# Two of a turn's 36 gathers replaced by columns copied on VectorE and ScalarE

## The chip, the cores and the metric

One core of a Trainium2 chip runs the whole program in one launch. The metric is the device time of one execution in microseconds. The kernel before takes 4103.11 us, the median of three runs (4102.42 to 4103.65).

## The reference

Two layers of a graph network over 6,250 nodes with 128 features and 206,250 directed edges, which are sorted by destination. The second layer, the convolution, is the one that the change is about. `src` and `dst` come from the inputs, so which rows are read is known only at run time.

```
h = max(layernorm(x), 0)
x = x + attention_layer(h, edge_index, edge_type, node_type, ...)     # layer 0: softmax over edges, 3 edge types
h = max(layernorm(x), 0)
filters    = silu(edge_attr @ fW1 + fb1) @ fW2 + fb2                  # per edge, 50 -> 128 -> 128
messages   = (h[src] @ dW + db) * filters                             # per edge
aggregated = segment_sum(messages, dst)                               # per node
x = x + (h + silu(aggregated @ uW1 + ub1) @ uW2 + ub2)
```

## The kernel before, in words

Edges are cut into chunks of 128 (one edge per partition), six chunks make a unit of 768 edges, six units make a turn. There are 269 units in 45 turns, the last of five units. Both layers run over the same turns, the attention layer first (`attention_edges`, line 721), then the convolution (`convolution_edges`, line 1300).

In the convolution the product `h @ dW + db` is not computed per edge. The attention layer's last steps write it, a row of 128 floats per node, to a table in HBM (`messages`, later `table`, line 799). It goes there 128 nodes at a time: once a turn from the third on, TensorE turns the tile of h (its features onto the partitions, `p.turned`, line 1079) and multiplies it by `dW`, VectorE adds `db` (line 1082, into the same buffer). The last seven tiles follow at the stage's end (line 814).

GpSimd then gathers, chunk by chunk, the rows of the 128 sources of a chunk into `xg` with one indirect DMA (`gather`, line 62, from `gather_units`, line 688): `xg` has a place for each of the six units of a turn, and a place is filled again as soon as VectorE has used it (`xg_free`, which is `s_msg`). Only one chunk in two turns (20 in all) doesn't come so: SyncE fetches its 128 rows by 128 single DMAs into a staging buffer (`Carry.collect`, lines 609 to 617) and moves them into the sixth chunk of unit 4. SyncE also loads the source indices, three units at a time (`load_indices`, line 620), after the units that used the old ones have landed.

The other engines in the convolution, per unit: TensorE makes the hidden layer (line 1441, two matmuls into `ps_h`), ScalarE applies silu (line 1387), TensorE makes the filters (line 1417, six matmuls into one of two PSUM banks), VectorE adds the bias `fb2` (line 1490) and multiplies by the gathered rows (line 1496), TensorE sums by destination (line 1426, with a one-hot that VectorE makes at line 1484), and VectorE adds the sums to the accumulator (line 1504). TensorE issues the hidden layer of unit n, then the filters of n-1, then the sums of n-3. Once a turn a finished tile of 128 nodes goes through the update layer (lines 1386, 1415, 1524, 1527) and out to HBM. ScalarE also issues the loads of the edge attributes, two a turn (line 1370). Each engine's order is written out by hand; nothing is planned at run time.

VectorE reads the window bases of a turn into registers by one load of ten values (line 500). The six loads of the residual `y` (448 KB each) are issued by SyncE in turn 0 (line 1354), three behind each index load.

Of the kernel before, what the change touches and what calls it, by code (L numbers as in the profile page):

```python
# [496 lines left out]

def bases(nc, engine, h, first, count):
# [40 lines left out]

LOAD = 3  # L540
# [15 lines left out]
def landed_by(pace, r, i, s, carried=0, j=0):  # L556
# [63 lines left out]
def load_indices(nc, sp, a, h, idx, idx_in, gathered, landed, carry, xg, xg_free, ahead=lambda r, i, v: None, beside=lambda r, i: None,  # L620
                 behind=lambda r, i: None, listed=lambda: None):
# [22 lines left out]
    def span(r, t, b, first=False):  # L644

        for q in range(span_turns * LOADS):
            j, v = divmod(q, LOADS)
            following(r, span_turns * t + j, v)
            if q == 0 and not first:
                deliver(r, t, b)  # L650
            if q == 0 and first:
                listed()
# [35 lines left out]
def gather_units(pool, passes, table, xg, width, idx, idx_in, gathered, xg_free, pool_turn, carry):  # L688
# [32 lines left out]
def attention_edges(nc, h, a, acc, state, typ, table, messages, sent, y, project, sources, following):  # L721

    with ExitStack() as ctx:
# [23 lines left out]
        landed, pool_turn, steps, key_ready, begun, rise_zero = (  # L747
            sem(k) for k in "landed pool_turn steps key_ready begun rise_zero".split())
# [32 lines left out]
        def _(sp):  # L781
# [21 lines left out]
            sp.sem_inc(stored, 32)  # L803
            load_indices(nc, sp, a, h, idx, idx_in, gathered, landed, carry, xg, s_sum, beside=beside, behind=behind)
# [4 lines left out]
            sp.wait_ge(stored, 32 * (passes * DONE + 1))  # L809
            first_indices(sp, a, following.idx, following.idx_in)  # L810
            for n, k in enumerate((1, 0)):
                a0, a1 = HALVES[k]
                sp.wait_ge(t_hdc, n + 1)
                sp.dma_start(messages[(LAST + a0) * P:(LAST + a1) * P, :].rearrange("(t p) r -> p t r", p=P), l_hd[:, a0:a1, :]).then_inc(last_stored, 16)
            sp.wait_ge(last_stored, 32)

        @block.gpsimd
        def _(pool):
            gather_units(pool, project.pool_passes, table, xg, ROW, idx, idx_in, gathered, s_sum, pool_turn, carry)
# [18 lines left out]
        def _(act):  # L838
            nc.scalar.copy(acc[:, 1:NT, 0:NP], acc[:, 0, 0:NP].unsqueeze(1).to_broadcast([P, NT - 1, NP]))
            with act.Fori(0, pass_count(act, h)) as r:  # L840
# [55 lines left out]
                def relus(k):  # L896

                    act.wait_ge(stored, 32 * k)
# [162 lines left out]
        def _(dve):  # L1061
# [9 lines left out]
            with dve.Fori(0, pass_count(dve, h)) as r:  # L1071
                def tile(i, s):
# [4 lines left out]
                    if closes(i) and s == 1:  # L1077
                        dve.wait_ge(stored, 32 * (r * DONE + i - OPEN))
                        nc.vector.tensor_copy(p.turned, ps_c[:, P:2 * P])
                        nc.vector.tensor_tensor(p.relu, p.rows, p.relu, ALU.add)  # L1080
                    if closes(i) and s == 2:
                        nc.vector.tensor_tensor(p.turned, ps_c[:, 2 * P:3 * P], p.db, ALU.add)
# [180 lines left out]
class Project:  # L1263


    def __init__(self, nc, ctx):
        sb = lambda name, shape: ctx.enter_context(nc.sbuf_tensor("pj_" + name, shape, fp32))
        self.w, self.dw, self.bias = sb("w", [P, NT, D]), sb("dw", [P, D]), sb("bias", [P, NT, D])
        parts = sb("parts", [P, 3, D])
        self.relu, self.turned, self.db = (parts[:, k, :] for k in range(3))  # L1270
# [4 lines left out]
        self.carry_turn = ctx.enter_context(nc.semaphore("pj_carry_turn"))  # L1275
        self.raise_from = self.tile[:, :, 0:TILES]
# [23 lines left out]
def convolution_edges(nc, h, a, acc, update, table, sent, sources, project, y, out):  # L1300

    with ExitStack() as ctx:  # L1302
# [17 lines left out]
        sem_landed = sem("landed")  # L1320
# [4 lines left out]
        (w_in, pool_turn, steps, key_ready, begun, cleared, s_hid, s_act, s_flt, s_bias, s_msg, s_sum, s_acc) = (  # L1325
            sem("c_" + k) for k in "w_in pool_turn steps key_ready begun cleared hid act flt bias msg sum acc".split())
# [6 lines left out]
        def _(sp):  # L1333
# [5 lines left out]
            update.load(sp, a)  # L1339

# [14 lines left out]
            load_indices(nc, sp, a, h, sources.idx, sources.idx_in, gathered, sem_landed, carry, xg, s_msg, attributes, beside=beside, listed=lambda: sp.wait_ge(scaled, 1))  # L1355
# [8 lines left out]
        def _(act):  # L1364
            act.wait_ge(w_in, 64)
            act.wait_ge(update.loaded, 64)
            with act.Fori(0, pass_count(act, h)) as r:
# [5 lines left out]
                def turn(i, first, count):  # L1373
                    for s in range(count):
# [6 lines left out]
                        if opens(i) and s == 1:  # L1381
                            k = r * DONE + i - OPEN
                            act.wait_ge(t_u, k + 1)
                            if not (isinstance(i, int) and i == OPEN):
# [3 lines left out]
                                             ACT.Silu, bias=fb1[:, :]).then_inc(s_act, 1)  # L1388
                finishing_turns(act, turn)
# [5 lines left out]
        @block.gpsimd  # L1395
        def _(pool):
            gather_units(pool, project.pool_passes, table, xg, D, sources.idx, sources.idx_in, gathered, s_msg, pool_turn, carry)

        @block.tensor
        def _(pe):  # L1400
            pe.sem_inc(s_hid, XS)
            pe.wait_ge(w_in, 64)
            pe.wait_ge(update.loaded, 64)
            with pe.Fori(0, pass_count(pe, h)) as r:
                def filters(n, s, fresh, i=None):
# [7 lines left out]
                    if i is not None and opens(i) and s == UPDATE_SLOT:  # L1413
                        pe.wait_ge(t_hid, r * DONE + i - OPEN + 1)
                        nc.tensor.matmul(tile_y, one_hid[:, :], update.w2[:, :], start=True, stop=True).then_inc(t_v, 1)
                    for c in range(CH):
# [3 lines left out]
                def sums(n, s, fresh, count=CH):  # L1420
# [6 lines left out]
                    last.then_inc(s_sum, 1)  # L1427

                def turn(i, first, count):
                    for s in range(count):  # L1430
# [12 lines left out]
                        if not (first and s < 1):  # L1443
                            filters(n - 1, (s - 1) % SL, first and s < 3, i if s else None)
# [27 lines left out]
        def _(dve):  # L1472
            dve.sem_inc(s_msg, XS)
            nc.vector.memset(h.sweep[:, :], 0.0).then_inc(cleared, 1)
# [6 lines left out]
            with dve.Fori(0, pass_count(dve, h)) as r:  # L1481
# [5 lines left out]
                def messages(n, s, i, carried, j=0):  # L1487
# [3 lines left out]
                    if s == UPDATE_SLOT and opens(i):  # L1491
                        update_tile(i)
                    dve.wait_ge(s_bias, n)
                    carry.landed(dve, r, s, carried)
                    dve.wait_ge(gathered[s], landed_by(carry.pace, r, i, s, carried, j))
# [10 lines left out]
                def turn(i, first, count, carried, j=0):  # L1506
                    back = 0 if first else 4
                    base = bases(nc, mybir.EngineType.DVE, h, i * SL - back, count - 4 + back)
                    for s in range(count):
# [3 lines left out]
                        if not (first and s < 1):  # L1513
                            one_hot(i * SL + s - 1, v)
                            messages(n - 1, v, i if s else i - 1, carried, j)
# [49 lines left out]
def program(nc, a, out):  # L1565
    table0 = nc.dram_tensor("table0", (NP, ROW), fp32).ap()
    sent = nc.dram_tensor("sent", (DONE * P, D), fp32).ap()
    table1 = nc.dram_tensor("table1", (NP, D), fp32).ap()
    with ExitStack() as ctx:
# [4 lines left out]
        with ExitStack() as banks:  # L1574
            with nc.sbuf_tensor("state", [P, NT, NW], fp32) as state, nc.sbuf_tensor("typ", [P, NU, CH], bf16) as typ:
                prepare(nc, h, a, sums, state, typ, table0, project, attention_sources)
                project.ring = banks.enter_context(nc.psum_tensor("ring", [P, 2048], fp32))
                attention_edges(nc, h, a, sums, state, typ, table0, table1, sent, y, project, attention_sources, sources)
        update = Update(nc, ctx)
        messages = sums[:, 0, :]  # L1580
        convolution_edges(nc, h, a, messages, update, table1, sent, sources, project, y, out)
# [43 lines left out]
```

## Time and profile before

| | us |
|---|---|
| median of three runs | 4103.11 |
| the profiled execution: its span, first to last instruction | 4098.5 |
| what lies around the span (4103.11 less 4098.5) | 4.6 |
| attention gathers, GpSimd | from 61.7 |
| convolution, first gather to the last sum | 2091.9 to 4090.9 |
| GpSimd busy, whole span | 3050.9 (74%) |
| TensorE busy | 3358.1 (82%) |
| VectorE busy | 2405.1 (59%) |
| ScalarE busy | 1368.9 (33%) |

Busy counts the instructions of the engines themselves; register loads and arithmetic, waits and the issue of DMAs are not in it. The profile has no time of its own for the execution beside its span, so 4.6 us is taken as what lies around it.

### The profile page before, as it was taken

Reading aid. Unit: us, or ns where it says so; the run is one execution under the profiler, and the core shown is the slowest. Engines: PE = TensorE matmul, PEld = TensorE weight load, DVE = VectorE, ACT = ScalarE, POOL = GpSimd, SP = SyncE. Lnnn points to the kernel's source line nnn. Section 1 sums busy time; section 2 is a strip of 40 time slices with the busy share of each in tenths; the row PEclk is TensorE's granted clock in tenths of the full one; section 3 lists DMA queues with packets and bytes.
Section 4 is the critical chain, followed back from the end, with each engine's and each line's share of the span. In section 5 each row is a group of like instructions: output and inputs, shape, how many; then the busy total and the mean of one; then the engine's idle time right before and its main releaser. Section 6 shows DMA issues by size and latency. Waiting matters only on the chain. (4 is left out here: it accounts for less than half of the span.)

```text
span 4098.5 us, 63699 instructions
## 1 busy us (share of the span) xinstructions
PE 3358.1 (82%) x14005; PEld 2625.3 (64%) x14006; DVE 2405.1 (59%) x5327; ACT 1368.9 (33%) x3398; POOL 3050.9 (74%) x3216
## 2 busy tenths in 40 slices
PE   5788888888888888888768898888888888888798
PEld 3566666666666666666656676766766666666676
DVE  7888888888888888888853333333333332333333
ACT  5455555555555555555421111111111111111111
POOL 6777777777777777777757777777777777777776
PEclk7555555555555555555567666667666677667767
DMA  4222222222222222222232222222222222222222
GB/s 125 58 60 61 61 60 61 62 60 61 61 60 61 61 61 60 61 61 59 59 88 78 79 74 78 79 74 78 75 77 78 75 78 78 74 79 74 78 78 62
DMA packets 190049, 288.10 MB, mean 70 GB/s; under 512 B 85904, under 2 KB 132811, under 8 KB 185384
## 3 DMA queue, kind: packets, MB, share of 16 engines
q0 software_dynamic: 101888, 212.13, 20.6%
q1 hardware_dynamic: 83160, 33.99, 3.5%
q10 hardware_dynamic: 4840, 40.55, 3.2%
q14 instruction: 147, 1.20, 0.1%
q8 instruction: 14, 0.23, 0.0%
HBM read 271.07 MB, written 12.49 MB: 69 GB/s over the span
## 5 line engine op out<-in xcount | busy, mean ns | idle before, releaser
L63 POOL DMA_INDIRECT ce_xg<-table,ce_idx x1592 | 1509.2, 948 | 491.6 <-issue 481.5
L63 POOL DMA_INDIRECT ae_xg<-table,ae_idx x1592 | 1502.5, 944 | 491.2 <-issue 489.6
L1496 DVE TENSOR_TENSOR ce_msg<-ce_ring,ce_xg 128x768 f32<-128x768 f32 x269 | 257.6, 958 | 1151.0 <-DMA ce_xg<-table,ce_idx 1150.6
L948 PE MATMUL ae_ps_k<-ae_xg,ae_e 128*96 128x129 f32 x3224 | 882.7, 432 | 0.0
L1417 PEld LDWEIGHTS ce_ring<-ce_fw,ce_hid 128*128 128x128 f32 x3228 | 586.6, 278 | 435.6 <-DVE ce_msg L1496 314.6
L1417 PE MATMUL ce_ring<-ce_fw,ce_hid 128*128 128x128 f32 x3228 | 649.6, 377 | 262.1 <-DVE ce_msg L1496 261.8
L948 PEld LDWEIGHTS ae_ps_k<-ae_xg,ae_e 128*96 128x96 f32 x3224 | 689.6, 277 | 126.7 <-issue 117.2
L1387 ACT ACTIVATE ce_hid<-ce_ps_h,ce_fb 128x768 f32<-128x768 f32 x269 | 241.8, 899 | 1235.4 <-PE ce_ps_h L1441 692.2
L1441 PE MATMUL ce_ps_h<-ce_ea,ce_fw 50*128 50x384 f32 x1076 | 548.3, 641 | 19.0 <-DMA ce_ea<-in_edge_attr 17.1
L1426 PEld LDWEIGHTS ce_ring<-ce_hot,ce_msg 128*128 128x128 f32 x3224 | 528.4, 253 | 3.0 <-DVE ce_msg L1496 2.9
L1426 PE MATMUL ce_ring<-ce_hot,ce_msg 128*128 128x32 f32 x3224 | 514.3, 319 | 1.0 <-DVE sums L1504 1.0
L868 ACT ACTIVATE ae_off<-cst,plan 128x96 bf16<-128x96 f32 x1614 | 454.1, 363 | 5.0 <-DVE plan L491 5.0
L860 ACT ACTIVATE ae_upper<-ring 128x576 f32<-128x576 f32 x269 | 174.9, 650 | 668.3 <-DVE ring L1125 668.3
L996 PE MATMUL ring<-ae_rise,cst 64*128 64x192 f32 x538 | 270.4, 605 | 84.2 <-DVE ae_rise L1148 81.2
L963 PE MATMUL ae_ps_tz<-cst,ae_high 128*96 128x128 f32 x269 | 120.7, 449 | 251.8 <-DVE ae_high L1135 251.8
L1441 PEld LDWEIGHTS ce_ps_h<-ce_ea,ce_fw 50*128 50x128 f32 x1076 | 227.2, 234 | 145.1 <-issue 65.8
L1135 DVE TENSOR_REDUCE ae_high<-ae_e 128x96 f32<-128x576 f32 x269 | 304.8, 1133 | 0.0
L1490 DVE TENSOR_TENSOR ce_ring<-ce_ring,ce_fb 128x768 f32<-128x768 f32 x269 | 258.3, 960 | 71.5 <-PE ce_ring L1417 71.2
L1125 DVE TENSOR_TENSOR ring<-ring,ae_xg 128x576 f32<-128x576 f32 x269 | 206.1, 766 | 126.0 <-DMA ae_xg<-table,ae_idx 122.3
L963 PEld LDWEIGHTS ae_ps_tz<-cst,ae_high 128*96 128x96 f32 x269 | 41.9, 156 | 316.6 <-DVE ae_high L1135 316.6
L996 PEld LDWEIGHTS ring<-ae_rise,cst 64*128 64x128 f32 x538 | 134.0, 308 | 171.4 <-DVE ae_rise L1148 158.2
L844 ACT ACTIVATE ae_e<-ae_e 128x576 f32<-128x576 f32 x269 | 183.7, 683 | 105.6 <-DVE ae_e L1157 105.5
(186 smaller groups left out, 3336.2 us busy)
## 6 DMA issues: line engine op xcount, KB each, us to landing
ae_stage<-table SPq DMA_DIRECT2D x2560, 0.5 KB
ce_stage<-table SPq DMA_DIRECT2D x2560, 0.5 KB
ce_ea<-in_edge_attr ACTq DMA_DIRECT2D x88, 450.0 KB
ae_xg<-table,ae_idx POOLq DMA_INDIRECT x1592, 2.5
ce_xg<-table,ce_idx POOLq DMA_INDIRECT x1592
sums<-in_x SPq DMA_DIRECT2D x7, 448.0 KB, 4.6
table<-sums SPq DMA_DIRECT2D x6, 462.0 KB, 3.5
pj_bias<-in_x_rows SPq DMA_DIRECT2D x42, 64.0 KB
```

The source lines that it names most:

```text
L63: eng.indirect_dma_start(out=out, out_offset=None, in_=table[:, :], in_offset=bass.IndirectOffsetOnAxis(ap=idx, axis=0)).then_inc(done, 16)
L868: last = nc.scalar.activation(off[:, s % 2, c, :], h.iota, ACT.Square, bias=keys[:, c:c + 1], scale=STEP)
L948: last = nc.tensor.matmul(ps_k[0:KEYS, 0:D + 1], by_chunk[s % 3][:, c, :], xg[:, s % XS, c, 0:D + 1], start=(c == 0), stop=(c == count - 1))
L996: nc.tensor.matmul(ps_m[s % 2][:, 0:2 * KEYS], h.raised_by[0:64, :], rise[:, :, :].rearrange("p a k -> p (a k)"), start=True, stop=True).t ...
L1125: nc.vector.tensor_tensor(by_kind, by_kind, xg[:, s % XS, :, D + 1:ROW].unsqueeze(3).to_broadcast([P, CH, NT, W]), ALU.add).then_inc(s_ful ...
L1135: nc.vector.tensor_reduce(out=high[:, :], in_=by_chunk[s % 3].rearrange("p c k -> p k c"), op=ALU.max, axis=AX.X).then_inc(s_high, 1)
L1387: nc.scalar.activation(hid[:, b, :].rearrange("p (k e) -> p k e", k=2), ps_h[:, :].rearrange("p (k e) -> p k e", k=2)[:, :, 0:H], ACT.Silu ...
L1417: last = nc.tensor.matmul(ps_f[b][:, c * D:(c + 1) * D], hid[:, b, c * P:(c + 1) * P], fw2[:, :], start=True, stop=True)
L1426: last = nc.tensor.matmul(ps_a[s % 2][:, 0:W], msg[:, s % 3, c, :], hot[:, s % 3, c, :], start=(c == 0), stop=(c == count - 1))
L1441: last = nc.tensor.matmul(ps_h[:, k * 512:k * 512 + H], fw1[:, :], ea[:, s // LOAD, q:q + H], start=True, stop=True)
L1490: nc.vector.tensor_tensor(filt, filt, fb2[:, :].unsqueeze(1).to_broadcast([P, CH, D]), ALU.add).then_inc(s_bias, 1)
L1496: nc.vector.tensor_tensor(msg[:, s % 3, :, :], filt, xg[:, s % XS, :, :], ALU.mult).then_inc(s_msg, 1)
```

## The change

In the convolution the sixth chunk of units 1 and 3 is no longer gathered in turns 2 to 44. Its h @ dW + db is computed afresh on the chip. For it h itself, turned, is written to HBM in the attention layer (`features`, [128, 6272] floats, one more DMA a turn and one at the end) and loaded whole into SBUF as `by_node` (3.2 MB, 25,088 bytes a partition) in turn 0 of the convolution. A source's h is then one column of `by_node`.

In each of turns 1 to 43, two blocks `held[:, m, :]` of 128 columns are filled: m = 0 in units 0 to 2 for unit 1 of the next turn, m = 1 in units 3 to 5 for unit 3. VectorE copies columns 0 to 47 (16 in each of three units), ScalarE columns 48 to 127 (28, 28 and 24). Each copy is an instruction of one element a partition, whose source address comes from a register; the registers are loaded from a list in SBUF (`columns`), up to 16 values by one load. TensorE multiplies the block by `dW` (one matmul of 128 columns), and VectorE adds `db` and writes the sum into `xg`.

```
+def sources_at(nc, engine, columns, i, m, first, end):
+    for e in range(first, end, PIECE):                      # PIECE = 16
+        yield from nc.values_load_multi_w_load_instructions(columns[32 * m:32 * m + 1, bass.ds((i - 1) * P + e, min(PIECE, end - e))], engines=[engine], ...)[1]

+COLUMNS = (Column((0, 1, 2), 5, 1), Column((3, 4, 5), 2, 3))    # collected in units, multiplied at, goes to unit
+COLUMN_TURNS = TURNS - 2
+HALF = 48

 gather_units:
-                taken = carried is not None and s == CARRY_SLOT
+                taken = carried is not None and s == CARRY_SLOT or s in to and not (isinstance(i, int) and i < 2)

 attention, SyncE:
-                    sp.dma_start(messages[bass.ds((i - OPEN - 1) * P, P), :], p.turned).then_inc(stored, 16)
+                    sp.dma_start(messages[bass.ds((i - OPEN - 1) * P, P), :], p.message).then_inc(stored, 16)
+                    sp.dma_start(features[:, bass.ds((i - OPEN - 1) * P, P)], p.turned).then_inc(stored, 16)
 ...
+            for ready in (t_ht, t_first_ht):
+                sp.wait_ge(ready, 1)
+            sp.dma_start(features[:, LAST * P:NP].rearrange("f (t p) -> f t p", p=P), l_ht).then_inc(project.last_turned, 16)

 convolution, SyncE, in turn 0 behind the first index load:
+            def tables(r):
+                sp.wait_ge(scaled, 1)
+                sp.wait_ge(project.last_turned, 16)
+                sp.wait_ge(s_column, r * COLUMN_TURNS * len(COLUMNS) + len(COLUMNS))
+                sp.dma_start(by_node, features[:, :]).then_inc(table_in, 16)

 convolution, ScalarE, behind the silu of each unit of turns 1 to 43:
+                def collect(i, s):
+                    e0, e1 = column.batch(s, HALF, P)
+                    if s == column.collected[0]:
+                        act.wait_ge(s_column, column_at(r, i, m) + 1)
+                    if s == 0:
+                        act.wait_ge(table_in, 16 * (r + 1 + len(COLUMNS)))
+                    for k, node in enumerate(sources_at(nc, mybir.EngineType.Activation, columns, i, m, e0, e1), e0):
+                        last = nc.scalar.copy(held[:, m, k:k + 1], by_node[:, bass.ds(node, 1)])
+                    if s == column.collected[-1]:
+                        last.then_inc(s_other, 1)

 convolution, TensorE, ahead of a unit's filters:
+                def products(i, m, b):
+                    pe.wait_ge(s_half, k + 1)
+                    pe.wait_ge(s_other, k + 1)
+                    nc.tensor.matmul(ps_x[b], held[:, m, :], project.dw[:, :], start=True, stop=True).then_inc(s_column, 1)

 convolution, VectorE, in messages(), between the bias and the multiplication by xg:
+                def collect(i, s):          # as ScalarE's, columns 0 to HALF, nc.vector.tensor_copy, s_half
+                def place(i, m, b):
+                    dve.wait_ge(s_column, column_at(r, i, m) + 1 + len(COLUMNS))
+                    dve.wait_ge(s_msg, r * UNITS + i * SL + column.to + 1 + XS)
+                    nc.vector.tensor_tensor(xg[:, column.to, CH - 1, :], ps_x[b], project.db, ALU.add).then_inc(s_placed, 1)
 ...
+                    for m, to in enumerate(TO):
+                        if s == to and not (isinstance(i, int) and i < 2):
+                            dve.wait_ge(s_placed, column_at(r, i - 1, m) + 2)
```

## Rows read from the trace of the kernel before

**Rows 1.** The page: busy time by engine, and the chain that ended last.
```profile
PE 3358.1 (82%) x14005; PEld 2625.3 (64%) x14006; DVE 2405.1 (59%) x5327; ACT 1368.9 (33%) x3398; POOL 3050.9 (74%) x3216
...
POOL 35%; issue 12%; DMA 1%; POOLq 1%; DVE 0%; PE 0%; ACT 0%; DVEq 0%
```

**Rows 2.** Timeline of POOL, 40 gathers apart: start us, duration us, instruction [idle before].
```profile
2999.86 0.94 POOL L63 DMA_INDIRECT ce_xg<-table,ce_idx  x1 [0.30 <-issue]
...
3049.83 0.95 POOL L63 DMA_INDIRECT ce_xg<-table,ce_idx  x1 [0.30 <-issue]
```

**Rows 3.** Groups of instructions on POOL, whole span.
```profile
L63 POOL DMA_INDIRECT ce_xg<-table,ce_idx x1592 | 1509.2, 948 | 491.6 <-issue 481.5 <-DVEq L1473 6.5 <-DVE ce_msg L1496 3.3
```

**Rows 4.** Who waited for whom, 2100 to the end: us, times, longest.
```profile
DVE ce_msg L1496 <- DMA ce_xg<-table,ce_idx: 1150.6, 264, 10.3
ACT ce_hid L1387 <- PE ce_ps_h L1441: 692.2, 144, 13.5
```

**Rows 5.** Busy time by engine in one turn: PE, PEld, DVE, ACT, POOL, clock, DMA.
```profile
3000.00:3044.30 44.30, 39.78 (x181) 31.15 (x180) 14.00 (x26) 6.56 (x8) 33.61 (x36) 0.69 0.30 82
```

**Rows 6.** Groups on DVE and ACT, 2200 to 4050 us.
```profile
L1524 DVE TENSOR_TENSOR ce_done<-sums,up_b 128x128 f32<-128x128 f32 x42 | 12.3, 293 | 77.8 <-DMA out_x<-ce_done 77.8
...
L1387 ACT ACTIVATE ce_hid<-ce_ps_h,ce_fb 128x768 f32<-128x768 f32 x250 | 224.7, 899 | 1145.2 <-PE ce_ps_h L1441 607.1 <-issue 538.1
```

**Rows 7.** Timeline of DVE: one unit, then a turn's start.
```profile
3020.20 0.96 DVE L1496 TENSOR_TENSOR ce_msg<-ce_ring,ce_xg 128x768 f32<-128x768 f32 x1 [7.78 <-DMA ce_xg<-table,ce_idx]
3021.07 0.18 DVE L1504 TENSOR_TENSOR sums<-sums,ce_ring 128x32 f32 x1
3021.17 0.35 DVE L1484 TENSOR_TENSOR ce_hot<-cst,key 128x192 f32<-128x192 f32 x1
3021.44 0.96 DVE L1490 TENSOR_TENSOR ce_ring<-ce_ring,ce_fb 128x768 f32<-128x768 f32 x1
3023.20 0.96 DVE L1496 TENSOR_TENSOR ce_msg<-ce_ring,ce_xg 128x768 f32<-128x768 f32 x1 [0.80 <-DMA ce_xg<-table,ce_idx]
3025.46 0.19 DVE L1504 TENSOR_TENSOR sums<-sums,ce_ring 128x32 f32 x1 [1.30 <-issue]
```

**Rows 8.** Register loads, by line: ns min/median/max, first and last start.
```profile
L500 DVEq TENSOR_LOAD <-base_i x1: 1412/1412/1412, 3023.7 to 3023.7; - x1
...
L500 DVEq TENSOR_LOAD <-base_i x46: 556/901/1429, 2109.7 to 4083.0; - x46
...
L613 SPq TENSOR_LOAD <-ce_lists x160: 1132/1208/1696, 2126.1 to 3881.8; - x160
```

**Rows 9.** Line 868 for one unit: sequencer's register work, and its instructions.
```profile
L868 ACTq FUSED_REGOPS  x6: 46/46/60, 1003.0 to 1003.6; - x6
```

**Rows 10.** Timeline of ACT: an activation of one column, and the next.
```profile
1000.56 0.20 ACT L894 ACTIVATE pj_few<-pj_few 128x1 f32<-128x1 f32 x1
1000.67 0.24 ACT L855 COPY ae_by_key<-ae_ps_k 96x129 f32<-96x129 f32 x1
```

**Rows 11.** Line 1146, a copy on DVE with a source address from a register.
```profile
L1146 DVE COPY ae_rise<-state x269: 240/241/243, 85.2 to 2058.5; 1x96 f32 x135
```

**Rows 12.** Groups on DVE: the shortest instruction.
```profile
L442 DVE MEMSET pr_eps<- 128x1 f32 x1 | 0.1, 59 | 0.0
```

**Rows 13.** Line 1370, the issue of ScalarE's attribute loads.
```profile
L1370 ACTq DMA_DIRECT2D ce_ea<-in_edge_attr x83: 731/738/763, 2208.9 to 4029.3; - x83
```

**Rows 14.** Timeline of SP in the convolution's first turns.
```profile
2124.39 1.68 SPq L1354 DMA_DIRECT2D sums<-sent  x3
2127.41 13.09 SPq L617 DMA_DIRECT2D ce_stage<-table  x32
2143.55 0.61 SPq L631 DMA_DIRECT2D ce_idx<-in_src  x1
```

**Rows 15.** Timeline of POOL: unit 3 of turn 1.
```profile
2147.78 0.94 POOL L63 DMA_INDIRECT ce_xg<-table,ce_idx  x1 [0.30 <-DMA ce_idx<-in_src]
```

**Rows 16.** Window behind the first loads of y, columns as in Rows 5, then GB/s.
```profile
2125.00:2130.00 5.00, 5.00 (x22) 4.63 (x22) 2.53 (x5) 0.14 (x1) 3.77 (x4) 0.50 0.89 237
```

More of the change, by code:

```diff
@@ L537, in __init__, with batch, collects, places @@
         self.chunks = (span * SL * np.arange(1, carried + 1) + CARRY_SLOT) * CH + CH - 1
+class Column:
+    def __init__(self, collected, placed, to):
+        self.collected, self.placed, self.to = collected, placed, to
+        self.late = placed < collected[-1]
+    def batch(self, s, e0, e1):
+        q, parts, fours = self.collected.index(s), len(self.collected), (e1 - e0) // 4
+        return e0 + 4 * -(-fours * q // parts), e0 + 4 * -(-fours * (q + 1) // parts)
+COLUMNS = (Column((0, 1, 2), 5, 1), Column((3, 4, 5), 2, 3))
+COLUMN_TURNS = TURNS - 2
+TO = [column.to for column in COLUMNS]
+HALF = 48
+PIECE = 16
+STORES = 48
+def collects(i):
+    return not (isinstance(i, int) and not 1 <= i <= COLUMN_TURNS)
+def places(i, column):
+    first = 2 if column.late else 1
+    return not (isinstance(i, int) and not first <= i < first + COLUMN_TURNS)
+def column_chunks():
+    turn = np.arange(2, TURNS)
+    return np.concatenate([(turn * SL + to) * CH + CH - 1 for to in TO])
+def column_at(r, i, m):
+    return r * COLUMN_TURNS * len(COLUMNS) + (i - 1) * len(COLUMNS) + m
 LOAD = 3
@@ L818, in _ @@
         def _(pool):
-            gather_units(pool, project.pool_passes, table, xg, ROW, idx, idx_in, gathered, s_sum, pool_turn, carry)
+            gather_units(pool, project.pool_passes, table, xg, ROW, idx, idx_in, gathered, s_sum, project.pool_turn, carry)
             pool.wait_ge(last_in, 16)
@@ L1297, with convolution_edges @@
 UPDATE_SLOT = 3
-def convolution_edges(nc, h, a, acc, update, table, sent, sources, project, y, out):
+def convolution_edges(nc, h, a, acc, update, table, features, by_node, sent, sources, project, y, out):
     with ExitStack() as ctx:
@@ L1324, in convolution_edges @@
         carry = Carry(sb, lambda name: sem("c_" + name), CONVOLUTION, D, project, lists, table)
-        (w_in, pool_turn, steps, key_ready, begun, cleared, s_hid, s_act, s_flt, s_bias, s_msg, s_sum, s_acc) = (
-            sem("c_" + k) for k in "w_in pool_turn steps key_ready begun cleared hid act flt bias msg sum acc".split())
+        (w_in, steps, key_ready, begun, cleared, s_hid, s_act, s_flt, s_bias, s_msg, s_sum, s_acc) = (
+            sem("c_" + k) for k in "w_in steps key_ready begun cleared hid act flt bias msg sum acc".split())
+        columns = sb("columns", [P, COLUMN_TURNS * P], i32)
+        held = sb("held", [P, len(COLUMNS), P])
+        ps_x = [ps_f[b][:, 1024 - P:1024] for b in range(2)]
+        table_in, s_half, s_other, s_column, s_placed = (sem("x_" + k) for k in "table_in half other column placed".split())
         merged, out_done, y_in, s_u, s_up_hid, s_v, s_up_bias, s_y = (sem("f_" + k) for k in "merged out_done y_in u hid v bias y".split())
@@ L1415, in filters @@
                         nc.tensor.matmul(tile_y, one_hid[:, :], update.w2[:, :], start=True, stop=True).then_inc(t_v, 1)
+                    for m, column in enumerate(COLUMNS):
+                        if at is not None and at[1] == column.placed and places(at[0], column):
+                            products(at[0] - 1 if column.late else at[0], m, b)
                     for c in range(CH):
@@ L1443, in turn @@
                         if not (first and s < 1):
-                            filters(n - 1, (s - 1) % SL, first and s < 3, i if s else None)
+                            filters(n - 1, (s - 1) % SL, first and s < 3, i if s else None, (i, s))
                         if not (first and s < 3):
@@ L1485, in one_hot, with aside, messages @@
                                             keys.unsqueeze(2).to_broadcast([P, CH, W]), ALU.is_equal)
-                def messages(n, s, i, carried, j=0):
+                def collect(i, s):
+                    m = next(m for m, column in enumerate(COLUMNS) if s in column.collected)
+                    column = COLUMNS[m]
+                    e0, e1 = column.batch(s, 0, HALF)
+                    if s == column.collected[0]:
+                        dve.wait_ge(s_column, column_at(r, i, m) + 1)
+                        dve.sem_inc(begun, 1)
+                    if s == 0:
+                        dve.wait_ge(table_in, 16 * (r + 1 + len(COLUMNS)))
+                        dve.sem_inc(begun, 1)
+                    for k, node in enumerate(sources_at(nc, mybir.EngineType.DVE, columns, i, m, e0, e1), e0):
+                        last = nc.vector.tensor_copy(held[:, m, k:k + 1], by_node[:, bass.ds(node, 1)])
+                    if s == column.collected[-1]:
+                        last.then_inc(s_half, 1)
+                def place(i, m, b):
+                    column = COLUMNS[m]
+                    dve.wait_ge(s_column, column_at(r, i, m) + 1 + len(COLUMNS))
+                    dve.wait_ge(s_msg, r * UNITS + i * SL + column.to + 1 + XS)
+                    nc.vector.tensor_tensor(xg[:, column.to, CH - 1, :], ps_x[b], project.db, ALU.add).then_inc(s_placed, 1)
+                def aside(r, at):
+                    if at is None:
+                        return
+                    i, s = at
+                    for m, column in enumerate(COLUMNS):
+                        if s == column.placed and places(i, column):
+                            place(i - 1 if column.late else i, m, (s - 1) % SL % 2)
+                    if collects(i):
+                        collect(i, s)
+                def messages(n, s, i, carried, j=0, at=None):
                     filt = ps_f[s % 2][:, 0:CH * D].rearrange("p (c f) -> p c f", c=CH)
```

66 lines of the change are left out of this document (43 added, 23 removed).

## The prediction

> **What bounds the kernel now.** I read the page first. TensorE is busiest by share, but the chain that ended last is 35% GpSimd and 12% "issue", and nothing else has over 1% [rows 1]. The reader should see that busy shares mislead here: the chain lies on GpSimd's indirect DMAs. The timeline of GpSimd says why: gathers follow each other with 0.94 us busy and 0.30 us "issue" between, and 40 of them take 49.97 us, so 1.249 us each [rows 2]. Over the whole convolution this hardly breaks: of 491.6 us of idle time before 1592 gathers, 481.5 are that issue time and 3.3 are waits for VectorE to free a place [rows 3]. The waits say the same from the other side: VectorE waits 1150.6 us for gathered rows, ScalarE 692.2 us for TensorE, which itself is held up by VectorE [rows 4]. So a turn costs 35.5 gathers (36, less one every second turn) x 1.249 = 44.3 us, and every other engine follows.
>
> **What is removed.** Units 1 and 3 lose one gather each in turns 2 to 44: 86 gathers x 1.249 = 107.4 us. A turn becomes 33.5 x 1.249 = 41.8 us. All of it is on the path, as long as no other engine needs over 41.8 us a turn. That is the whole question, and I work out each engine's turn.
>
> **ScalarE, 80 x 2 = 160 copies a turn.** No such copy is in the trace. An instruction whose address comes from a register first takes register work of the sequencer: six at line 868 start within 0.6 us though each takes 0.046, so one every 0.12 to 0.13 us, the dispatch included [rows 9]. On the engine itself an activation of one column lasts 0.20 us and the next starts 0.11 us after it [rows 10]. Low end 0.11, high end 0.20 (no overlap). I take 0.13, since the sequencer feeds no faster: 160 x 0.13 = 20.8. Register loads: two per unit, 16 values and 12 (8 in every third). SyncE's loads of 16 have a median of 1.21, VectorE's of ten 0.90 [rows 8]; so 1.21 + 0.90 = 2.1 a unit, 12.7 a turn. Two attribute loads are issued at 0.74 [rows 13], with their registers 1.7. The update tile, loop and semaphore waits: I allow 1.6. Sum 36.8 us. The six silus of 0.90 [rows 6], 5.4 us, run on the engine while the sequencer loads the next registers: on VectorE a load started at 3023.7 [rows 8] while the multiplication of 3023.20 to 3024.16 still ran [rows 7]. Without that cover it is 42.2, just over GpSimd's turn. With 0.20 a copy, its loads and silus not hidden: 32 + 12.7 + 5.4 + 3.3 = 53.4.
>
> **VectorE, 48 x 2 = 96 copies.** Its bounds lie further apart: 0.06 (the one-column memset) [rows 12] and 0.24 (a copy with a register address, 96 elements on one partition) [rows 11]. I take 0.13 as on ScalarE: 12.5 us. Six loads of 16 at 1.21: 7.3. Today's work by start spacing: 0.87 + 0.10 + 0.27 + 0.96 = 2.2 a unit, 13.2 a turn [rows 7]. Base load 1.4, update tile 0.6 plus its wait for the store before, 77.8 / 42 = 1.9 [rows 6], two `place` additions 0.6. Sum 37.5 us with nothing overlapped, against 41.8. At 0.24 a copy it would be 48.1, which is over.
>
> The copies stand ahead of the multiplication by `xg`. What is queued behind them is that multiplication; for it wait TensorE's sums and GpSimd's next gather into the place, six units on. A unit's 3.3 us come while rows are still landing, where VectorE idles 7.8 us in one unit and 0.8 in the next [rows 7]. GpSimd's lead of several units takes up the uneven landing.
>
> **TensorE.** Two more matmuls of 128 columns a turn. It is busy 39.8 of 44.3 us at a granted clock of 0.69, between its two levels of 1.2 and 2.4 GHz [rows 5]. The same work must now fit into 41.8; at 0.69 it does, with about 0.8 us for the two: 40.6. The new waits there (`s_half`, `s_other`) are for units collected two to three units earlier, and cost nothing. Cover is thin: at a mean clock of 0.60 it would need about 47.
>
> **SyncE and the beginning.** In turn 0 the 3.2 MB of `by_node` go behind the first three loads of `y` and ahead of the staging rows. Those 1.34 MB are mostly in a window of 5 us at 237 GB/s, the gathers' bytes included [rows 16]. At 240 to 350 GB/s the table takes 9 to 13 us more, in which gathers hardly land. The index load for unit 3 of turn 1 waits for unit 5 of turn 0 to land; it was issued at 2143.55 and GpSimd needed it just as it came, at 2147.78, with no more than the usual 0.30 between gathers [rows 14, 15]. Any delay there goes straight to the path. I estimate 3.5 us: gathers held until about 2142, then a backlog of some 5 us. VectorE's and ScalarE's wait for the table at turn 1 is behind that and within GpSimd's lead. Low end 0, high end 13.
>
> In the attention layer SyncE gets one more DMA a turn (about 0.4 us) while GpSimd sets the pace, so nothing; at its end two waits and one more DMA stand ahead of the last wait for the stores: 1 us. The renamed and shared semaphores cost nothing.
>
> **The sum.** Span 4098.5 - 107.4 + 3.5 + 1.0 = 3995.6; with 4.6 us around it 4000.2. The profiled execution has no other time of its own, and by this account it equals the median of 4103.11. So **4000 us, 2.5% faster**.
>
> A rule of the Trainium skill weighs against the VectorE part. First the rows: the copy at line 1146, float from SBUF to SBUF, took 240 to 243 ns in all 269 cases [rows 11] beside a GpSimd that was busy three quarters of the time, so none of them waited for a gather's 0.94 us. "SBUF — State Buffer", section "SBUF: two separate sides", says that a VectorE copy in a two-port mode and GpSimd's descriptor writing exclude each other for a whole instruction. By the rule the new copies would queue behind gathers; by the row they don't. Another, "VectorE: DVE Perf Modes", section "The TRN2 errata", gives a ScalarE instruction from SBUF to SBUF 224 cycles at 1.2 GHz; 160 x 0.19 = 30 us a turn would, as an estimate by that page, bring ScalarE to about 46, where the overlap in rows 10 says less.
>
> **Rivals.**
> *(a) Part of the gain is lost (0.13).* ScalarE or VectorE need 42 to 44 us a turn: silus uncovered (42.2), or code for 160 copies fetched anew each turn. Each us over 41.8 costs 43: at 43 us a turn 4000 + 52 = 4052. For it: the thin margins above. Against: 5 us of margin on ScalarE, 4 on VectorE.
>
> *(b) ScalarE becomes the bound (0.09), slower.* A one-column copy takes its full 0.20 us and nothing hides the loads: 53.4 us a turn, (53.4 - 44.3) x 43 = +391, so 4494. With the loads hidden it is about 44 to 46 and the time 4100 to 4180. It decides from (44.3 - 12.7 - 5.4 - 3.3) / 160 = 0.143 us a copy without cover. For it: no row shows one of these copies. Against: rows 9 and 10.
>
> *(c) VectorE's copies and GpSimd's gathers take turns (0.06), slower.* Copies run only in the 0.30 us between gathers [rows 2]. At 0.06 each [rows 12] five fit, so 16 need four gaps, 5.0 us; with 1.2 and 2.2 a unit takes 8.4, a turn 50.4: +262, so 4365. Against: rows 11.
>
> *(d) Nothing changes (0.03)*: one engine happens to need 44 to 44.5 us.
>
> The forecast has 0.69. **Range and chances.** The forecast's own range is 3994 (no delay at the beginning, a little overlap gained) to 4013 (the full 13 us). Reaching into (a) up to 4085 holds about eight in ten: 3993 to 4085. About 0.2% (8 us) is what a measurement of this kernel tells from no change. Faster: the forecast and nearly all of (a), 0.81; same 0.04; slower, (b) and (c), 0.15.
>
> **What would show it.** Line 63 in the convolution has 1506 gathers and still 1.249 us between them, with no new releaser. ScalarE's and VectorE's copies start 0.11 to 0.14 us apart within a batch. VectorE's wait for gathered rows falls from 1150 us to 200 to 500 but doesn't vanish; if it is near zero and GpSimd waits for line 1496's successor, (a), (b) or (c) holds, and the copies' spacing tells which: over 0.14 on ScalarE is (b), copies on VectorE that start in clusters after gathers end is (c). One idle stretch of GpSimd before unit 3 of turn 1 is the table's price. The prediction is wrong if a turn of GpSimd takes over 42.5 us.

## The result, and the profile after

The changed kernel takes 3995.99 us (median of four runs, 3994.69 to 3998.18) against 4103.38 us of the kernel before beside it: a ratio of 0.9736, with a 95% interval of 0.9723 to 0.975. Its profiled execution spans 3994.3 us, 104.2 less than the 4098.5 before.

The page after, busy times and the chain of waits, which answer to [rows 1]:
```profile
PE 3385.6 (85%) x14177; PEld 2645.2 (66%) x14178; DVE 2914.9 (73%) x9541; ACT 2120.9 (53%) x10279; POOL 2970.5 (74%) x3130
...
POOL 32%; issue 11%; DMA 2%; DVE 1%; POOLq 1%; DVEq 1%; PE 0%; SPq 0%
```
VectorE and ScalarE are busy for 1262 us more in sum (509.8 and 752.0), and the chain is still GpSimd's (in c0_after's profile, further down, 23% GpSimd and 11% TensorE). The costliest groups that answer to [rows 3, 6, 7], from the page:
```profile
L63 POOL DMA_INDIRECT ce_xg<-table,ce_idx x1506 | 1429.0, 949 | 465.6 <-issue 454.0
L1473 ACT COPY ce_held<-sums 128x1 f32 x6880 | 751.9, 191 | 329.3 <-issue 325.2
...
L1598 DVE COPY ce_held<-sums 128x1 f32 x4128 | 507.5, 153 | 118.7 <-issue 117.8
```
1592 gathers have become 1506, of unchanged length. Their timeline, 40 gathers apart, answers to [rows 2] (start, duration, instruction, idle before):
```profile
2998.64 0.94 POOL L63 DMA_INDIRECT ce_xg<-table,ce_idx  x1 [0.30 <-issue]
...
3048.74 1.09 POOL L63 DMA_INDIRECT ce_xg<-table,ce_idx  x1 [0.30 <-issue]
```
50.10 us for 40, against 49.97 before; one gather of 1.09 us at 3006.13 in place of 0.94 makes up all of the difference. One turn answers to [rows 5]; the columns are the same:
```profile
3000.00:3041.80 41.80, 36.09 (x172) 28.78 (x172) 24.75 (x118) 23.50 (x173) 31.73 (x34) 0.74 0.31 80
```
Who waited for whom, 2095 us to the end, answers to [rows 4]:
```profile
ACT ce_hid L1456 <- issue: 381.6, 120, 6.3
...
DVE ce_msg L1633 <- DMA ce_xg<-table,ce_idx: 298.2, 109, 7.5
DVE sums L1641 <- issue: 170.1, 41, 6.0
ACT ce_hid L1456 <- PE ce_ps_h L1539: 118.0, 54, 10.1
```
VectorE's wait for gathered rows fell from 1150.6 us to 298.2. It is the room that the new copies use: it shrank and did not vanish. GpSimd's waits for VectorE to free a place stay at 4.0 us from 2200 to 3800 us, 3.3 before. ScalarE's timeline over most of a turn shows how the copies come:
```profile
3003.80 0.90 ACT L1456 ACTIVATE ce_hid<-ce_ps_h,ce_fb 128x768 f32<-128x768 f32 x1
3005.03 1.71 ACT L1473 COPY ce_held<-sums 128x1 f32 x16 [0.32 <-issue]
3007.54 1.30 ACT L1473 COPY ce_held<-sums 128x1 f32 x12 [0.81 <-issue]
3008.90 1.27 ACTq L1439 DMA_DIRECT2D ce_ea<-in_edge_attr  x1
...
3014.26 0.90 ACT L1473 COPY ce_held<-sums 128x1 f32 x8 [0.56 <-issue]
3018.96 0.90 ACT L1456 ACTIVATE ce_hid<-ce_ps_h,ce_fb 128x768 f32<-128x768 f32 x1 [3.81 <-issue]
```
Sixteen copies of 0.19 us take 1.71 us together: each starts (1.71 - 0.19) / 15 = 0.101 us after the one before. Between batches stands what is left of a register load, 0.81 us. At the turn's end ScalarE stands still for 3.81 us with nothing but "issue" as the reason. VectorE's timeline of one unit:
```profile
3001.82 0.96 DVE L1623 TENSOR_TENSOR ce_ring<-ce_ring,ce_fb 128x768 f32<-128x768 f32 x1
3002.69 1.92 DVE L1598 COPY ce_held<-sums 128x1 f32 x16
3005.08 0.96 DVE L1633 TENSOR_TENSOR ce_msg<-ce_ring,ce_xg 128x768 f32<-128x768 f32 x1 [0.47 <-DMA ce_xg<-table,ce_idx]
```
Here the spacing is (1.92 - 0.15) / 15 = 0.118 us, right through two of GpSimd's gathers:
```profile
3002.39 0.94 POOL L63 DMA_INDIRECT ce_xg<-table,ce_idx  x1 [0.30 <-issue]
3003.64 0.94 POOL L63 DMA_INDIRECT ce_xg<-table,ce_idx  x1 [0.30 <-issue]
```

**Where the 104.2 us come from.** 86 gathers give 107.4. Against it stand the first gather, 0.74 us later than before (2092.68 for 2091.94), 1.6 us more between the last gather's start and the end (14.7 us, from 3979.58, for 13.1 from 4085.35), and 0.9 us of small irregularities between gathers. In a second profiled execution of the same kernel (c0_after below) the last gather starts at 3977.77 of a span of 3990.9, so 13.1 us again. In e1, e2, e3, e5 and e9 it is 13.5 to 14.8, with 14.8 in e1, which has none of the one-column copies: it varies from one execution to the next, and the 1.6 can't be put down to the change.

### The profile page after: what moved, and what is told of

It reads as the page before. It is cut to its first block and busy times, and to the rows that moved or that the text cites. A ratio compares the mean times of both kernels' runs of the same rounds, so it can differ in the third digit from the quotient of the medians.

```text
span 3994.3 us, 88540 instructions
## 1 busy us (share of the span) xinstructions
PE 3385.6 (85%) x14177; PEld 2645.2 (66%) x14178; DVE 2914.9 (73%) x9541; ACT 2120.9 (53%) x10279; POOL 2970.5 (74%) x3130
## 5 line engine op out<-in xcount | busy, mean ns | idle before, releaser
L63 POOL DMA_INDIRECT ce_xg<-table,ce_idx x1506 | 1429.0, 949 | 465.6 <-issue 454.0
L1473 ACT COPY ce_held<-sums 128x1 f32 x6880 | 751.9, 191 | 329.3 <-issue 325.2
L1508 PEld LDWEIGHTS ce_ring<-ce_fw,ce_hid 128*128 128x128 f32 x3228 | 594.9, 281 | 156.3 <-issue 90.8
L1598 DVE COPY ce_held<-sums 128x1 f32 x4128 | 507.5, 153 | 118.7 <-issue 117.8
L1539 PE MATMUL ce_ps_h<-ce_ea,ce_fw 50*128 50x384 f32 x1076 | 561.5, 655 | 34.0 <-DMA ce_ea<-in_edge_attr 19.1
L1517 PEld LDWEIGHTS ce_ring<-ce_hot,ce_msg 128*128 128x128 f32 x3224 | 509.7, 245 | 6.2 <-DVE ce_msg L1633 2.9
L1517 PE MATMUL ce_ring<-ce_hot,ce_msg 128*128 128x32 f32 x3224 | 496.7, 312 | 4.1 <-DVE sums L1641 2.5
L1633 DVE TENSOR_TENSOR ce_msg<-ce_ring,ce_xg 128x768 f32<-128x768 f32 x269 | 257.6, 958 | 305.1 <-DMA ce_xg<-table,ce_idx 298.2
L1018 PEld LDWEIGHTS ae_ps_tz<-cst,ae_high 128*96 128x96 f32 x269 | 41.8, 155 | 320.3 <-DVE ae_high L1190 320.3
```

What stands on the lines that cost most here:

```text
L63: eng.indirect_dma_start(out=out, out_offset=None, in_=table[:, :], in_offset=bass.IndirectOffsetOnAxis(ap=idx, axis=0)).then_inc(done, 16)
L1473: last = nc.scalar.copy(held[:, m, k:k + 1], by_node[:, bass.ds(node, 1)])
L1508: last = nc.tensor.matmul(ps_f[b][:, c * D:(c + 1) * D], hid[:, b, c * P:(c + 1) * P], fw2[:, :], start=True, stop=True)
L1517: last = nc.tensor.matmul(ps_a[s % 2][:, 0:W], msg[:, s % 3, c, :], hot[:, s % 3, c, :], start=(c == 0), stop=(c == count - 1))
L1539: last = nc.tensor.matmul(ps_h[:, k * 512:k * 512 + H], fw1[:, :], ea[:, s // LOAD, q:q + H], start=True, stop=True)
L1598: last = nc.vector.tensor_copy(held[:, m, k:k + 1], by_node[:, bass.ds(node, 1)])
```

## The experiments

The kernel before ran beside each: 4102.77 us (13 runs, 4099.38 to 4107.8) beside the first eight, 4102.16 in one run beside the last two. Where no interval is given a kernel ran once.

**c0_after: the changed kernel again.** No edit.

> The changed kernel again, timed on the same chip as the three runs beside it. Theory (GpSimd sets the pace, 86 gathers of 1.249 us are gone, all else is hidden): 3996 us, within 3 us. Rival (part of the 107.4 us is given back by slower turns, which varies from run to run): more than 5 us of scatter.

Measured 3993.74 us (3991.11 to 3995.28), ratio 0.9731 [0.9714, 0.9747].

**e1_block: the copies without their addresses.** Each batch becomes one copy of a fixed block, without register loads. The messages of the two chunks are then not their sources'.
```
-                    for k, node in enumerate(sources_at(nc, ..., columns, i, m, e0, e1), e0):
-                        last = nc.scalar.copy(held[:, m, k:k + 1], by_node[:, bass.ds(node, 1)])
+                    last = nc.scalar.copy(held[:, m, e0:e1], by_node[:, e0:e1])      # and so on VectorE
```


> The register loads and the 256 one-column copies a turn are left out: each engine copies its share of a block in one instruction, columns 0 to 127 of the table in place of the sources' (so the messages of those two chunks are not those of their sources). Waits, matmuls, additions and dropped gathers stay. Theory (the copies and loads are hidden entirely): 3994 to 3997, no faster than with them; the jump back at a turn's end falls from 2.75 us (VectorE) and 3.2 to 4.0 us (ScalarE) to some 0.1 us, since the turn's code is short again; the last gather to the end is back at 13.2 us from 14.8. Rival (they cost part of the gain): 3970 to 3990.

Measured 3996.64 us (3994.89 to 3999.79), ratio 0.974 [0.9724, 0.9757]: the same as with all 256 copies. Everything that they cost lies beside GpSimd's work. The end did not come back to 13.2 us as expected, it is 14.8. Groups of this kernel, then of the changed one, 2200 to 3800 us, show what became of the stall at a turn's end, which falls before VectorE's addition of the sums:
```profile
L1639 DVE TENSOR_TENSOR sums<-sums,ce_ring 128x32 f32 x229 | 41.0, 179 | 47.7 <-issue 36.8 <-PE ce_ring L1516 10.8
```
```profile
L1641 DVE TENSOR_TENSOR sums<-sums,ce_ring 128x32 f32 x229 | 41.1, 180 | 168.4 <-issue 168.4
```
Before the change this "issue" is mostly the base load (1.30 us a turn in [rows 7]), and so it is here: 36.8 us over 38 turns is 1.0 a turn. In the changed kernel it is 168.4 / 38 = 4.4. So 3.4 us a turn on VectorE come with the 96 copies and six loads in the loop's body and go with them. The records of the sequencers where the changed kernel's loop jumps back show where it lies (within 3000 to 3042 us; count, ns, first and last start):
```profile
L526 ACTq COMPARE_BRANCH  x1: 54/54/54, 3015.0 to 3015.0; - x1
L526 ACTq FUSED_REGOPS  x1: 119/119/119, 3018.7 to 3018.7; - x1
...
L627 DVEq COMPARE_BRANCH  x2: 55/59/63, 3020.2 to 3020.3; - x2
L627 DVEq MOVE  x2: 36/40/43, 3023.1 to 3023.2; - x2
```
Behind the jump back ScalarE's sequencer does nothing for 3.6 us and VectorE's for 2.8. In e1 neither of them pauses there for over 0.3 us, from 2200 to 3800. The page lists a DMA queue of the kind "instruction" (packets, MB, share of the engines); the changed kernel, then e1:
```profile
q14 instruction: 547, 4.48, 0.4%
```
```profile
q14 instruction: 156, 1.28, 0.1%
```
The kernel before has 147. So 400 packets of 8 KB come with the copies and go with them. In the changed kernel four packets lie in ScalarE's pause (3015.3 to 3019), two in VectorE's idle stretch (3021 to 3025.8), none from 3003 to 3015. That each pause is a fetch of the loop's code fits count, time and place; the queue's row doesn't say which engine a packet is for, so that last step is argued.

**e2_kept: the new work, and the gathers too.** GpSimd gathers all 36 chunks again, and the sum with `db` goes to a tile that nothing reads.
```
-gather_units(..., project.pool_turn, carry, TO)
+gather_units(..., project.pool_turn, carry)
-nc.vector.tensor_tensor(xg[:, column.to, CH - 1, :], ps_x[b], project.db, ALU.add)
+nc.vector.tensor_tensor(aside_x[:, :], ps_x[b], project.db, ALU.add)
```


> All the new work is done, but GpSimd gathers all 1592 chunks and the computed messages go to a tile that nobody reads. Theory (adds nothing to a turn of 44.3 us): before plus 0.7 us at the convolution's beginning plus up to 1.6 at its end, 4104 to 4106. Rival (the new work slows GpSimd's gathers or starves a unit now and then): 4110 or more.

Measured 4102.09 us (4100.06 to 4106.82, 10 runs), ratio 0.9999 [0.9989, 1.0008]. The table's write and load, 256 copies, two products and two additions a turn cost nothing that can be measured; all the gain is the removed gathers.

**e3_one: one column instead of two.**
```
-COLUMNS = (Column((0, 1, 2), 5, 1), Column((3, 4, 5), 2, 3))
+COLUMNS = (Column((0, 1, 2), 5, 1),)
```


> Only the first of the two chunks is taken from GpSimd (unit 1's; units 3 to 5 copy nothing). Theory: 43 gathers of 1.249 us go, 53.7 us, less 0.8 us at the beginning and up to 1.6 at the end: 4050 to 4052. Rival (a first column is free, a second pays partly): below 4047, since then the first one brings more than half.

Measured 4048.61 us (4046.55 to 4054.66), ratio 0.9863 [0.9846, 0.9879]. The first column gives 54.2 us, the second another 54.9, against 43 gathers of 1.249 = 53.7 each; e3's own runs lie 8 us apart. The gain is linear in gathers up to here.

**e4_act_twice and e5_dve_twice: every copy made twice, on one engine.** In e4 on ScalarE (320 a turn), in e5 on VectorE (192).
```
+for to in (twice, held):
+    last = nc.scalar.copy(to[:, m, k:k + 1], by_node[:, bass.ds(node, 1)])      # e5: nc.vector.tensor_copy
```


> ScalarE copies each of its columns twice (the first time into a tile that nobody reads): 320 copies a turn, the register loads unchanged. The changed kernel's trace has 16 of its copies in 1.71 us, so 0.10 each, and a ScalarE turn of about 36 us with the jump back. Theory (0.10 a copy, sequencer and engine overlapped): 36 + 16 = 52 us a turn, so (52 - 44.3) x 43 above before: about 4440. Rival one (the 0.13 of the prediction): 57.6 us, about 4670. Rival two (a copy's full 0.19 us, if nothing overlapped): 67 us, about 5080.

> VectorE copies each of its columns twice (once into a tile that nobody reads): 192 copies a turn. In the trace 16 take 1.92 us, 0.118 each, and a unit takes 4.0 us of VectorE. Theory: 31 + 11.3 = 42 us a turn, on the edge of GpSimd's 41.8: 3996 to 4020. Rival (VectorE's turn is already nearly full, the 37.5 of the prediction without overlap): 49 us, about 4300.

Measured: e4 4022.83 us, e5 3999.86. e5 is inside what was expected, though not for the reason given; e4 is a plain miss, by some 400 us. Its timeline of ScalarE:
```profile
3002.13 0.19 ACT L1475 COPY ce_twice<-sums 128x1 f32 x1
3002.23 0.19 ACT L1475 COPY ce_held<-sums 128x1 f32 x1
3002.32 0.19 ACT L1475 COPY ce_twice<-sums 128x1 f32 x1
```
and its groups, 2200 to 3800 us:
```profile
L1475 ACT COPY ce_held<-sums 128x1 f32 x5986 | 1110.5, 188 | 0.0
L1475 ACT COPY ce_twice<-sums 128x1 f32 x5986 | 1110.4, 188 | 78.6 <-issue 71.0
```
Copies now start every 0.093 us on average, and the idle time before them is 78.6 us where the changed kernel has 288.8 in the same window. The second copy of a source needs no new address. ScalarE's sequencer gets ahead of its engine, and does the loads and address work of the next copies while the engine still works the old ones off. So the two don't add up, the longer one counts: the expectation had charged a doubled copy like a new one. GpSimd did lose here: the turn went from 41.8 to 41.8 + (4022.8 - 3993.7) / 43 = 42.5 us, with ScalarE waiting almost only for itself (busy 1334.85 of 1600 us, the fourth engine in the row below). By this it is the sequencer that sets ScalarE's turn in the changed kernel, not the copies' execution.
```profile
2200.00:3800.00 1600.00, 1425.46 (x6597) 1127.25 (x6597) 983.76 (x4641) 1334.85 (x12234) 1203.56 (x1274) 0.71 0.31 80
```
e5's timeline of VectorE shows the same there:
```profile
2999.87 0.15 DVE L1600 COPY ce_twice<-sums 128x1 f32 x1
2999.94 0.14 DVE L1600 COPY ce_held<-sums 128x1 f32 x1
3000.02 0.15 DVE L1600 COPY ce_twice<-sums 128x1 f32 x1
```
From 2200 to 3800 its copies start 0.076 us apart on average, the changed kernel's 0.120. 192 x 0.076 is 14.6 us and 96 x 0.120 is 11.5: the doubling cost some 3 us a turn and not the 11.3 of the expectation, so VectorE was never at the edge, and the hit is luck.

**e6_half16 and e7_half96: the split between the engines.** Sources, addresses and loads move with the copies.
```
-HALF = 48
+HALF = 16        # e7: 96
```


> Another split: VectorE copies 16 columns of a block, ScalarE 112. ScalarE's turn gains 64 copies at 0.10 and six more register loads (18 in all; 5.6 us): 36 + 12 = 48 us. Theory: ScalarE becomes the bound, (48 - 44.3) x 43 above before, 4260 within 60. Rival (ScalarE's loads are hidden by its engine's backlog): 43 us a turn, 4050.

> The other way: VectorE copies 96 columns of a block (32 a unit, two loads), ScalarE 32. VectorE's turn gains 96 copies at 0.118 and six loads at 1.1: 31 + 18 = 49 us. Theory: VectorE becomes the bound, 4300 within 60; ScalarE idles. Rival (the loads are hidden under the bias addition): 43 to 45 us a turn, 4050 to 4130.

Measured: e6 4242.57 us, e7 4405.48. e6 hit, e7 came 45 us beyond its upper end. The waits of e6, then of e7, 2200 to 3800 us:
```profile
DVE ce_ring L1623 <- PE ce_ring L1508: 900.7, 198, 9.5
ACT ce_held L1473 <- issue: 401.7, 667, 1.1
...
POOL ce_xg L63 <- DVE ce_msg L1633: 202.0, 123, 3.5
...
PE ce_ps_h L1539 <- ACT ce_hid L1456: 137.0, 81, 3.5
```
```profile
ACT ce_hid L1456 <- PE ce_ps_h L1539: 517.4, 93, 10.9
...
DVE ce_held L1598 <- issue: 309.1, 365, 1.2
...
POOL ce_xg L63 <- DVE ce_msg L1633: 298.9, 104, 6.6
```
In both, GpSimd now waits for VectorE to free a place (202.0 and 298.9 us; [rows 3] had 3.3). In e6 VectorE is not the cause, for it waits 900.7 us for TensorE's filters; TensorE in turn waits for ScalarE's silus, which stand behind 224 copies a turn, and ScalarE's own idle time is nearly all "issue"; in e7 VectorE has 192 copies and waits for next to nothing. A turn is 44.3 + (4242.6 - 4102.8) / 43 = 47.6 us on ScalarE, and 44.3 + (4405.5 - 4102.8) / 43 = 51.3 on VectorE. From the changed kernel's estimated 36 and 31 that is 11.6 us for 64 copies and six loads on ScalarE (18 loads a turn for 12; by 0.101 and 0.81: 11.3), and 20.3 for 96 copies and six loads on VectorE (by 0.118 and 1.1: 17.9). The 36 is borne out, the 31 was too low. From 2200 to 3800 us, 38.3 turns, the changed kernel's VectorE waits for TensorE and DMAs for 324.5 us:
```profile
DVE ce_msg L1633 <- DMA ce_xg<-table,ce_idx: 226.6, 84, 7.5
...
DVE ce_ring L1623 <- PE ce_ring L1508: 81.1, 45, 3.7
DVE ce_done L1661 <- DMA out_x<-ce_done: 16.8, 16, 7.2
```
That is 8.5 us a turn and leaves 33.3 of 41.8; 33.3 + 17.9 = 51.2 is what e7 took. Sixteen copies also often take longer than the 1.92 us above, as in e7:
```profile
3006.77 2.04 DVE L1598 COPY ce_held<-sums 128x1 f32 x16 [1.20 <-issue]
```
This isn't e7's own, the changed kernel has the like:
```profile
3027.76 2.04 DVE L1598 COPY ce_held<-sums 128x1 f32 x16 [0.55 <-issue]
```

**e8_three and e9_half64: is there anything left to win?** e8 takes three columns of two chunks, with 56 copies each on VectorE; e9 keeps two with an even split.
```
-COLUMNS = (Column((0, 1, 2), 5, 1), Column((3, 4, 5), 2, 3))
+COLUMNS = (Column((0, 1), 4, 0), Column((2, 3), 1, 1), Column((4, 5), 2, 3))
-HALF = 48
+HALF = 56        # e9: COLUMNS as it was, HALF = 64
```


> Three columns of two chunks each in place of two of three: 384 copies a turn for 256, and one gather a turn fewer on GpSimd (33.3 for 34.3 with the rest). The first 56 copies of a column are VectorE's, 72 ScalarE's. If GpSimd were still what ends a turn, the turn would be 41.8 - 1.25 = 40.6 us, and the time about 3994 - 43 x 1.25 = 3940. If the turn is what the copying engines can bear, VectorE goes from 31 us by 72 copies of 0.118, six register loads of 1.1 and one more placing of 0.3 to 46.4, and ScalarE from 36 by 56 copies of 0.10 and five loads of 0.8 to 45.6, besides what they wait for each other: a turn of 46 to 49, a time of 4103 + 43 x (47.5 - 44.3) = 4240, between 4170 and 4310.

> The same two columns, with 64 copies of each on VectorE and 64 on ScalarE (48 and 80 in the changed kernel): 32 copies and two register loads a turn more on VectorE, as many fewer on ScalarE. VectorE's turn goes from 31 to 31 + 32 x 0.118 + 2 x 1.1 = 37.0 us, ScalarE's from 36 to 31.2, both below GpSimd's 41.8. If GpSimd sets the time, this is 3994, within 6. If either copying engine set part of it, the time would move by 43 turns times what the split shifts: 43 x 1 us a turn is 43 us, and under 3980 or over 4020 would be read so.

Measured: e8 4277.77 us, a turn of 48.4; e9 3997.99; both are inside what was expected. The split can move by 16 columns to VectorE without effect; a third column costs far more than its gather. e9 did more than its expectation says: VectorE has six register loads a turn more (516 in 43 turns for 258), not two, and ScalarE as many as before. It waits for others 90.3 us from 2200 to 3800, 2.4 a turn, where the changed kernel has 8.5. The waits of e8, 2200 to 3800 us:
```profile
ACT ce_held L1473 <- issue: 383.6, 673, 1.2
...
DVE ce_held L1598 <- issue: 286.6, 330, 1.9
POOL ce_xg L63 <- DVE ce_msg L1633: 259.0, 109, 6.5
```
Both copying engines are at their limit at once. No version tried beats the changed kernel by more than its runs differ.

## Why the prediction was right

Forecast 4000.2 with 3995.6 for the span; measured 3995.99 and 3994.3. That the span is met within 1.3 us is in part luck: the 3.5 us at the beginning were not spent, and 1.6 at the end and 0.9 between gathers, for which the sum has no term, took their place. In c0_after, whose span is 3990.9, nothing did, and the forecast is 4.7 too high. And what lies around the span is 1.9 us and not 4.6 (3996.17 less 3994.3 here; 4101.18 less 4099.3 in a run of the kernel before): the forecast had subtracted one execution's span from the median of others. Point by point:

- **GpSimd sets a turn, 86 gathers go: right.** 107.4 us were forecast from the spacing; the spacing stayed, and e3 gives 54.2 and 54.9 for the two halves. e1 and e2 close it from both sides: without the copies' cost nothing is gained, with it and all gathers nothing is lost.
- **The beginning, 3.5 us: wrong, it cost nothing.** The table's load went where it was said, but the index load that I called critical was not.
```profile
2125.95 4.50 SPq L1408 DMA_DIRECT2D sums<-features  x1
...
2149.22 0.61 SPq L683 DMA_DIRECT2D ce_idx<-in_src  x1
```
```profile
2163.55 0.94 POOL L63 DMA_INDIRECT ce_xg<-table,ce_idx  x1 [0.30 <-issue]
```
  The index load came 5.7 us later than in [rows 14]. Yet unit 3 of turn 1 begins with gather 55 of the convolution, the row of 2163.55 (before the change it starts at 2162.76). The gather at 2147.78, which the prediction took for it, is the 43rd, the first of unit 1. I had taken the releaser named in [rows 15] for a need. The idle time there was the usual 0.30 us, so nobody had waited. The load was issued 14.3 us before its first use.
- **The end of attention, 1 us: right in size** (0.74, and 0.39 in c0_after).
- **ScalarE's turn, 36.8: right in sum, by errors that cancel.** A copy costs 0.10 and not 0.13 (-4.8 us a turn), a load costs less where the silu covers it, but the stall at the turn's end costs 3.8 us, which had no term, and the issue of an attribute load 1.27 instead of 0.74. From the timeline I count about 36 us, an estimate, and e6 gives 47.6 - 11.3 = 36.3. The cover of the silus was there: the silu of 3003.80 ends at 3004.70 and the copies behind it start 0.32 us later, with their sixteen registers loaded.
- **VectorE's turn, 37.5: high.** 0.118 a copy, and the overlap of loads with the wide additions, which I left out, give less: about 31 by my count of the timeline, 33.3 by its waits and e7, with 3.4 us of jump stall in it. The unoverlapped sum made the margin look like 4 us where it was 8.5; e9 used 6.1 of them without loss.
- **TensorE at a clock of 0.69: right.** 36.1 busy us at a granted 0.74 in the turn shown, 1459.7 / 38.3 = 38.1 a turn at 0.70 from 2200 to 3800 us (0.69 before), where 40.6 were forecast; the warning about 0.60 didn't come true.
- **Rival (a), part lost by code fetched anew: a stall of its kind is there**, 3.4 us a turn on VectorE and 3.8 on ScalarE, and the margins take it.
- **Rival (b), ScalarE the bound: out as priced**, since copies start 0.10 apart and not 0.20. It comes true 64 copies later (e6). The point from which it decides, 0.143 us a copy without cover, was not tested.
- **Rival (c), copies and gathers take turns: out.** 16 VectorE copies ran on for 1.92 us through gathers of 0.94. The prediction weighed two pages of the Trainium skill. "SBUF — State Buffer", section "SBUF: two separate sides", speaks of VectorE copies in a two-port mode that exclude GpSimd. These copies show no exclusion; no row tells in which mode they ran. By the 224 cycles of "VectorE: DVE Perf Modes", section "The TRN2 errata", a ScalarE copy would take 0.187 us, an estimate from the page's figure. The trace has just that as its duration, 0.19, but one starts every 0.10, so the page's number is a latency here and not a price.

The signs that were named in advance came as named: 1506 gathers, still 1.249 apart but for a few, no new releaser, a wait for rows between 200 and 500 (298), except the copy spacing of ScalarE, just below the band of 0.11 to 0.14.

## What to carry to other kernels

When one engine issues the work that bounds a kernel and the others idle behind it, a removed instruction there is worth its full spacing, and the cost of the replacement counts only once another engine's turn passes the bound. So work out every engine's turn against the new bound, not its busy share. In these runs an engine works at two paces, that of its sequencer (addresses, register loads, DMA issue, the jump back) and that of its execution; the longer of the two counts, and only the second shows as busy. So count the instructions in a loop's body too: past some length the jump back cost 2.8 to 4 us here. Before a releaser in a row is read as a tight deadline, look whether the idle time in front of it is longer than in the rows beside it.

## What the runs showed of the hardware that I had not expected

- One-column copies with a register address overlap on both engines: ScalarE 0.191 us long and 0.101 apart (0.093 where the address is reused), VectorE 0.153 long and 0.126 apart, some 0.06 in the first ones behind a wide instruction, which makes 0.118 to 0.126 in a batch (0.076 on average where every second address is reused).
- The new register loads, ns (min, median, max), read 16 values on VectorE and 16, 12 or 8 on ScalarE. VectorE's sixteen take 1.10 us, less than the ten values that took up to 1.43 in [rows 8]:
```profile
L501 ACTq TENSOR_LOAD <-ce_columns x516: 544/960/1232, 2145.7 to 3940.2; - x172
...
L501 DVEq TENSOR_LOAD <-ce_columns x258: 1095/1101/1136, 2145.7 to 3938.7; - x129
```
- Past some length of a loop's body the sequencer pauses behind the jump back. The time from the end of the jump's record to the sequencer's next one, median from 2200 to 3800 us, by the copies in the engine's loop:

| engine | no pause over 0.3 us | pause |
|---|---|---|
| VectorE | 0 (before, e1), 32 (e6), 48 (e3) copies | 96 copies 2.8 to 2.9 us, 128 (e9) 2.8, 192 (e5, e7) 2.8 to 2.9 |
| ScalarE | 0 (before, e1), 64 (e7), 80 (e3), 128 (e9) copies | 160 copies 3.9 to 4.1 us, 224 (e6) 2.6 |

  So it sets in between 48 and 96 copies, with their register loads, on VectorE and between 128 and 160 on ScalarE, and a still longer body doesn't make it longer. e3, which has no pause, has 164 "instruction" packets, nearly as few as the kernel before. Two runs stand apart: in e4, with 320 copies in ScalarE's loop (pause 3.7), VectorE with its 96 pauses for 6.5 us, and in e8, with 168 and 216, the pauses are 3.3 and 2.5. What one engine's fetches cost the other was not tried by itself.
